# Graph attention, experts and slice attention on one core: chain rows are scattered to a table with one row per node, and router scores are made from raw rows

## The chip, the cores and the metric

One core of a Trainium2 chip runs the whole program. The metric is the device time of one execution in microseconds (us). The engines are PE (TensorE), DVE (VectorE), ACT (ScalarE), POOL (GpSimd) and SP (SyncE); SP, ACT and POOL also issue transfers (DMAs).

## The reference

Two layers, each a graph stage and a dense stage, on 3125 nodes of 256 features, with 50,000 edges sorted by destination:

```python
# layer 0, graph: attention over edges, 8 heads of 32, plus a self loop per node
e = leaky_relu(a_src[src] + a_dst[dst], 0.2)
e = exp(e - segment_max(e, dst)[dst])
alpha = e / segment_sum(e, dst)[dst]
out = segment_sum(xh[src] * alpha, dst) + bias
out = (out - mean(out, 0)) * rsqrt(var(out, 0) + eps) * gamma + beta
x = x + out + ...                                      # residuals
# layer 0, dense: router over 8 experts, top 2 of softmax
xn = layernorm(x); probs = softmax(xn @ router_w.T)
x = x + sum over the top 2 experts of gate * w2(silu(w1 xn) * w3 xn)
# layer 1: sums of source rows per node, then slice attention
```

## The kernel before, in words

The program is a row of blocks, each of which ends with a barrier of all engines: `first_phase`, `spread_phase`, `edge_phase`, `join_phase`, `router_phase`, `experts_phase`, and then the second layer. Inside a block each engine's order is written out by hand, and semaphores tie them together. `me(dve, ...)` is a step on DVE that waits for its own end before the next.

The edges are cut into ET = 392 tiles of 128 (EP). `edge_phase` makes for every edge position running sums within its tile and stores them in the table `parts` (272 numbers a row: 256 sums, 8 denominators, 8 maxima). A node whose edges end in a tile has its sums in one row of `parts`, the main row; if its edges began in an earlier tile, what came before has to be carried over tile borders.

`join_phase` does that. It loads the last row of every tile (`lasts`), lays them out with 8 heads or 128 features on the partitions, runs scans over the 392 tiles on DVE (maxima, denominators, sums), and turns the result back into `carried`, 98 x 4 rows. Before the change `carried` is stored as `chains`, 392 rows and one neutral row. POOL gathers for each node its main row (25 indirect DMAs of 125 nodes, `join_main`) and then its chain row (25 more, `join_chain`); a node without a chain reads the neutral row. The node's own message (`join_xh`, `own`) and its main row are weighted and added first, with weights of their own (`early`, in PSUM), then chain rows come in and all is rescaled. Five groups of TB = 5 tiles of 125 nodes (P) make up the 25 tiles (NT); one DVE instruction handles a group, 1280 elements. Then mean and variance over nodes are summed on PE with a matrix of ones, and the features go into the residual `res`.

`move` issues a transfer over 125 partitions as two DMAs, of 120 and of 5 partitions.

`router_phase` takes statistics of `res` (`norm_stats`), makes normalized rows (`r_xn`) on DVE, stores them for the experts (`xn_tab`), and per node tile turns the rows on PE, copies them on ACT and multiplies by the turned router weights (`rwt`): `logits`. Softmax, top 2 and the slot lists of the experts follow on DVE.

`first_phase` makes the row numbers (`main_row`, `chain_row`, `start_row`) at its end. `spread_phase` has POOL scatter and gather (25 + 4 + 28 indirect DMAs) while PE and ACT turn the first expert's weights (`w_raw`, `w_stage`).

Of the kernel before, what the change touches and what calls it, by code (L numbers as in the profile page):

```python
# [40 lines left out]
NO_CHAIN = ET  # L41
# [64 lines left out]
def setup(k):  # L106
# [28 lines left out]
    k.chains = k.dram("chains", [ET + 1, RW])  # L135
# [9 lines left out]
def first_tables(k, ctx):  # L145
# [3 lines left out]
    k.chain_rows = k.sb("chain_row", [128, NT], I32, ctx)  # L149
# [7 lines left out]
    k.main_row, k.chain_row = k.main_rows[0:P, :], k.chain_rows[0:P, :]  # L157
# [8 lines left out]
def first_phase(k):  # L166
# [4 lines left out]
    with ctx:  # L171
# [15 lines left out]
        last_i, has, t0, t1 = sb("last_i", [P, NT], I32), sb("has", [P, NT]), sb("t0", [P, NT]), sb("t1", [P, NT])  # L187
# [40 lines left out]
        def _(sp):  # L228
# [20 lines left out]
            sp.dma_start(k.chains[NO_CHAIN:NO_CHAIN + 1, :], dummy[:, :]).then_inc(dummies_out, 16)  # L249
            sp.wait_ge(dummies_out, 32)  # L250
# [33 lines left out]
        def _(pool):  # L284
# [7 lines left out]
            for rows in (tiles_i[:, :], k.main_rows[:, :], k.chain_rows[:, :], k.places[:, :, :]):  # L292
                nc.gpsimd.memset(rows, 0)
# [57 lines left out]
        def _(dve):  # L351
# [66 lines left out]
            for t in range(NT):  # L418
# [11 lines left out]
            me(dve, v.tensor_copy(last_i[:, :], last[:, :]))  # L430
            me(dve, v.tensor_single_scalar(tile_i[:, :], last_i[:, :], 7, ALU.logical_shift_right))
            me(dve, v.tensor_copy(tile[:, :], tile_i[:, :]))


            v.tensor_scalar(t0[:, :], last[:, :], -float(NO_ROW), None, ALU.add)
            me(dve, v.scalar_tensor_tensor(out=t1[:, :], in0=tile[:, :], scalar=float(EP), in1=start[:, :],
                                           op0=ALU.mult, op1=ALU.is_gt))
            v.tensor_tensor(t0[:, :], t0[:, :], has[:, :], ALU.mult)
            me(dve, v.tensor_tensor(t1[:, :], t1[:, :], has[:, :], ALU.mult))
            v.tensor_scalar(k.main_row[:, :], t0[:, :], float(NO_ROW), None, ALU.add)  # L440
            me(dve, v.tensor_scalar(tile[:, :], tile[:, :], -1.0 - NO_CHAIN, None, ALU.add))
            me(dve, v.tensor_tensor(t1[:, :], t1[:, :], tile[:, :], ALU.mult))
            v.tensor_scalar(k.chain_row[:, :], t1[:, :], float(NO_CHAIN), None, ALU.add)
# [134 lines left out]
def spread_phase(k):  # L578
# [4 lines left out]
    with ctx:  # L583
# [4 lines left out]
        own0 = sb("own0", [P, NT, H])  # L588
        firsts_in = k.gather_sem("firsts_in")
# [6 lines left out]
        @block.sync  # L596
        def _(sp):
            for m in range(3):
                w.load(sp, 0, NE - 1, m)
            for m in range(3):  # L600
                w.store(sp, 0, NE - 1, m)
                w.load(sp, 1, 0, m)
            sp.wait_ge(starts_out, 16 * NT)
            sp.dma_start(sparse[:, :], edge_rows).then_inc(sparse_in, 16)

# [27 lines left out]
        def _(act):  # L633
            act.wait_ge(w.cleared, 1)
# [8 lines left out]
        def _(dve):  # L643
            v = nc.vector
            w.clear()
            st["dve"](dve, v.tensor_tensor(own0[:, :, :], k.xh[:, :, C:C + H], k.xh[:, :, C + H:RW], ALU.add))
# [495 lines left out]
def gather_rows(pool, into, table, row, rows_in):  # L1142

    for t in range(NT):
# [4 lines left out]
def join_phase(k):  # L1149
# [7 lines left out]
    w = RW  # L1157
    with ctx:
# [4 lines left out]
        sum_t = [sb(f"sum_t{c}", [128, ET]) for c in range(2)]  # L1163
        den_t, max_t, den_c, max_c, neg, keep, scale = (sb(n, [H, ET]) for n in ("den_t", "max_t", "den_c", "max_c", "neg", "keep", "scale"))
        xh = sb("xh", [P, NT, C])
        mains, chains = sb("main", [128, NT, RW]), sb("chain", [128, NT, RW])
        main, chain = mains[0:P, :, :], chains[0:P, :, :]
        top1, top, tmp = sb("top1", [P, NT, H]), sb("top", [P, NT, H]), sb("tmp", [P, NT, H])
        den1, den = sb("den1", [P, NT, H]), sb("den", [P, NT, H])
        gap, wt = sb("gap", [P, 2, NT, H]), sb("wt", [P, 2, NT, H])  # L1170
        rowv = sb("rowv", [P, 2, C])
        mean, var = sb("mean", [P, C]), sb("var", [P, C])
        mains_in, chains_in = k.gather_sem("join_mains_in"), k.gather_sem("join_chains_in")
        lasts_in, turned, drops, factors, spread, scanned, back, rows_made, stored = (
            sem(n) for n in ("lasts_in", "turned", "drops", "factors", "spread", "scanned", "back", "rows_made", "stored"))
# [4 lines left out]
        early = k.ps[5][0:P, 0:2 * NT * H].rearrange("p (a t h) -> p a t h", a=2, h=H)  # L1180
# [1147 lines left out]
```

## Time and profile before

| | us |
|---|---|
| median of three runs | 2132.3 (2129.28 to 2139.41) |
| the profiled execution | 2129.41 |
| its span | 2127.5 |
| PE busy | 1339.4 (63%) |
| DVE busy | 926.3 (44%) |
| POOL busy | 1127.4 (53%) |
| join, from its start to its end | 666 to 808 |
| router | 808 to 894 |
| experts | 894 to 1270 |

The profiled execution took 1.9 us more than its span, which is what lies around it, and 2.9 us less than the median. The stages follow from the barriers between the blocks. In a row of a timeline the bracket at its end is the time for which the engine had been idle and what ended that.

### The profile page before, as it was taken

What the parts mean: (1) busy time and instruction counts of PE and PEld (TensorE: products, weight loads), DVE (VectorE), ACT (ScalarE), POOL (GpSimd) and SP (SyncE); (2) the same over time, 40 slices, a digit from 0 to 9 for tenths busy, and PEclk for the clock granted to TensorE, in tenths of its full rate; (3) what the DMA queues carried; (4) which work ended last, traced back from release to release, by engine and by line L of the source; (5) the groups of instructions that cost most, each with busy time, mean ns of one, the idle gap of its engine ahead of it and who ended that gap; (6) DMA issues with size and microseconds to landing.
All of it is one profiled execution on the core that took longest, in us unless ns stands there. A gap on an engine that the chain in (4) does not pass through costs nothing. (4 is left out here: it accounts for less than half of the span.)

```text
span 2127.5 us, 23423 instructions
## 1 busy us (share of the span) xinstructions
PE 1339.4 (63%) x6378; PEld 1096.7 (52%) x6378; DVE 926.3 (44%) x1854; ACT 436.9 (21%) x1241; POOL 1127.4 (53%) x1105
## 2 busy tenths in 40 slices
PE   2612666656663155399999995055656566587878
PEld 1412544444443045399999995044444444464557
DVE  8613443454452675733333333733333333255543
ACT  0112544334442012133333331000000000012210
POOL 3376777777774600277322372177777777703320
PEclk6756888777776575599999997577778777789999
DMA  5444998888888703143111023633333333300002
GB/s 133 129 132 133 299 309 259 277 286 291 265 281 226 107 0 102 28 143 94 42 47 69 28 95 81 169 105 105 104 107 104 107 104 105 105 11 0 0 1 60
DMA packets 150672, 268.29 MB, mean 126 GB/s; under 512 B 23662, under 2 KB 112186, under 8 KB 149437
## 3 DMA queue, kind: packets, MB, share of 16 engines
q0 software_dynamic: 47136, 126.92, 20.9%
q1 hardware_dynamic: 89985, 126.37, 18.3%
q10 hardware_dynamic: 13438, 13.56, 3.0%
q8 instruction: 63, 1.03, 0.2%
q14 instruction: 50, 0.41, 0.1%
HBM read 172.94 MB, written 94.74 MB: 126 GB/s over the span
## 5 line engine op out<-in xcount | busy, mean ns | idle before, releaser
L1080 POOL DMA_INDIRECT sum_rows<-xn_tab,src_e x392 | 371.7, 948 | 174.2 <-issue 116.1
L1101 PE MATMUL bank<-sum_rows,sum_hot 128*125 x896 | 291.1, 496 | 257.3 <-SPq L1071 241.5
L721 POOL DMA_INDIRECT gat_rows<-xh_tab,src_e x364 | 348.1, 956 | 116.2 <-issue 109.1
L1101 PEld LDWEIGHTS bank<-sum_rows,sum_hot 128*125 128x125 f32 x896 | 218.2, 252 | 327.4 <-issue 282.8
L793 PE MATMUL bank<-gat_rows,gat_same 128*128 128x264 f32 x784 | 267.6, 483 | 138.4 <-issue 138.4
L793 PEld LDWEIGHTS bank<-gat_rows,gat_same 128*128 128x128 f32 x784 | 175.5, 243 | 179.2 <-issue 148.1
L1127 DVE TENSOR_TENSOR sums<-sums,bank 125x256 f32 x224 | 94.4, 421 | 337.1 <-PE bank L1101 334.8
L1688 PE MATMUL bank<-weights,e_xthigh 128*128 x896 | 220.5, 330 | 8.3 <-DVE e_xtlow L1805 5.4
L837 ACT COPY gat_outs<-bank 128x264 f32<-128x264 f32 x392 | 148.5, 380 | 249.5 <-PE bank L793 243.5
L1810 DVE TENSOR_TENSOR e_h<-e_gated,bank 128x342 f32<-128x342 f32 x112 | 57.1, 510 | 263.2 <-ACT e_gated L1758 263.2
L1688 PEld LDWEIGHTS bank<-weights,e_xthigh 128*128 128x128 f32 x896 | 154.2, 192 | 18.1 <-issue 17.9
L1688 PE MATMUL bank<-weights,e_xtlow 128*128 x448 | 144.9, 324 | 0.0
L1709 PE MATMUL bank<-weights,e_hthigh 128*128 (+2 forms) x672 | 133.5, 294 | 0.3 <-DVE e_htlow L1815 0.3
L758 DVE TENSOR_TENSOR gat_rows<-gat_rows,bank 128x1792 f32<-128x1792 f32 x56 | 110.4, 2013 | 0.5 <-ACT bank L829 0.5
L1592 POOL CAST weights<-staged 128x4264 fp32r<-128x4264 f32 x7 | 26.3, 3761 | 152.0 <-SPq L1637 143.0
L1709 PEld LDWEIGHTS bank<-weights,e_hthigh 128*128 128x128 f32 (+2 forms) x672 | 102.6, 189 | 0.5 <-issue 0.5
L1758 ACT ACTIVATE e_gated<-bank 128x342 f32<-128x342 f32 x112 | 51.0, 456 | 239.8 <-PE bank L1688 239.8
L1709 PE MATMUL bank<-weights,e_htlow 128*128 x336 | 94.1, 280 | 0.0
L1688 PEld LDWEIGHTS bank<-weights,e_xtlow 128*128 128x128 f32 x448 | 85.8, 192 | 0.0
L742 DVE TENSOR_TENSOR gat_logit<-gat_rows,adst_e 128x112 f32<-128x112 f32 x28 | 7.7, 276 | 153.4 <-DMA gat_rows<-xh_tab,src_e 153.4
L2032 POOL TENSOR_TENSOR t_logit<-t_logit,t_peak 125x512 f32<-125x512 f32 x25 | 26.1, 1045 | 82.7 <-DVE t_peak L2191 82.7
L1653 POOL DMA_INDIRECT y_tab<-e_x,slot_row x52 | 50.6, 973 | 34.7 <-ACT e_x L1768 20.3
(463 smaller groups left out, 2303.2 us busy)
## 6 DMA issues: line engine op xcount, KB each, us to landing
parts<-gat_outs SPq DMA_DIRECT2D x28, 1904.0 KB, 8.1
staged<-w_tab SPq DMA_DIRECT2D x8, 2132.0 KB, 8.4
w_tab<-w_stage SPq DMA_DIRECT2D x16, 682.0 KB, 10.5
w_raw<-in_L_ffn_w_dram SPq DMA_DIRECT2D x16, 640.0 KB
gat_rows<-xh_tab,src_e POOLq DMA_INDIRECT x392, 4.5
sum_rows<-xn_tab,src_e POOLq DMA_INDIRECT x392, 2.8
w_tab<-w_stage SPq DMA_DIRECT2D x8, 768.0 KB, 10.5
w_raw<-in_L_ffn_w_dram SPq DMA_DIRECT2D x8, 682.0 KB, 11.3
```

Of the source, the lines that this page charges most:

```text
L721: pool.indirect_dma_start(out=rows[b % R][:, t, :], out_offset=None, in_=k.xh_tab, in_offset=bass.IndirectOffsetOnAxis(ap=k.src_e[:, b * S ...
L758: v.tensor_tensor(f, f, weight[b % 2][:, t0 * H:t1 * H].rearrange("p (t h a) -> p t h a", h=H, a=1).to_broadcast([EP, SB // 2, H, D]), ALU ...
L793: nc.tensor.matmul(k.ps[1 + n % BK][:, 0:sums_w], same[b % 2][:, t, :], rows[b % R][:, t, 0:sums_w], start=True, stop=True).then_inc(sums, 1)
L837: nc.scalar.copy(outs[b % 2][:, t, 0:sums_w], k.ps[1 + n % BK][:, 0:sums_w]).then_inc(taken, 1)
L1080: pool.indirect_dma_start(out=rows[:, at // IP % (RING * GPAIRS), at % IP, :], out_offset=None, in_=k.xn_tab, in_offset=bass.IndirectOffse ...
L1101: m = nc.tensor.matmul(k.ps[s][0:P, 0:C], hot[u][:, s, c, :], rows[:, bass.ds(slot, 1), c, :].rearrange("p a c -> p (a c)"), start=(c == 0 ...
L1127: v.tensor_tensor(into, into, k.ps[s][0:P, 0:C], ALU.add).then_inc(added, 1)
L1653: pool.indirect_dma_start(out=k.y_tab, out_offset=bass.IndirectOffsetOnAxis(ap=k.slot_row[:, i:i + 1], axis=0), in_=k.x_row(i), in_offset= ...
L1688: last = nc.tensor.matmul(bank[:, 0:HH[a]], xt[s][px][:, c, :], part(slot, up_at(m, pw, c) + HB[a], 128, HH[a]), start=(n == 0), stop=(n = ...
L1709: m = nc.tensor.matmul(DOWN[s][:, 0:C], ht[a][ph][0:rows, b, :], part(slot, down_at(pw, 3 * a + b), rows, C), start=(a == 0 and n == 0), s ...
L1758: nc.scalar.activation(gated[a][:, 0:HH[a]], UP[a][:, 0:HH[a]], ACT.Silu).then_inc(silued, 1)
L1810: v.tensor_tensor(h[a][:, 0:HH[a]], gated[a][:, 0:HH[a]], GATE[a][:, 0:HH[a]], ALU.mult).then_inc(h_made, 1)
```

## The change

1. The table `chains` is gone. In its place is `node_chain`, one row for each of the 3125 nodes. ACT fills it in `spread_phase` with neutral rows, from an SBUF row `empty` (3125 rows of 1088 bytes, 3.4 MB). `join_phase` scatters `carried` to it, four indirect DMAs on POOL, and then loads it whole into `join_chain` with plain DMAs: tiles 0 to 12 from SP, 13 to 24 from ACT.
2. The node that each tile's chain belongs to (`chain_node`) is found in `spread_phase` by two matmuls, nine short DVE steps on one partition, four transposes and a copy. `first_phase` loses the eight DVE instructions for `chain_row`, a memset and one small DMA.
3. POOL issues 18 gathers of main rows, waits for `carried`, issues the four scatters, then the other 7 gathers.
4. The early weights are gone: all three terms get their weights once chain rows are there, with one exponential of 600 columns instead of two of 400.
5. The load of `join_xh` waits for `lasts`.
6. The router weights are loaded in the join, centred over their columns and turned at its head. The scores are made from raw rows of `res` at the end of the join, group by group behind the last DVE passes, and are multiplied by `rstd` in the router. The statistics move into the join too, and ACT's square root for them stands behind its 25 copies.
7. The normalized rows are made on ACT in the router, after the exponential, 25 instructions, instead of on DVE.

```diff
 # spread_phase
+            act.wait_ge(empty_made, 2)
+            move(act, k.node_chain.rearrange("(t p) c -> p t c", p=P), empty[:, :].rearrange("p (a c) -> p a c", a=1).to_broadcast([P, NT, RW]), k.chain_cleared)
             act.wait_ge(w.cleared, 1)
...
+            me(dve, v.tensor_tensor(whole[:, :], whole[:, :], follows[:, 1:1 + ET], ALU.mult))
+            me(dve, v.tensor_scalar(whole[:, :], whole[:, :], -1.0, 1.0, ALU.mult, ALU.add))
+            me(dve, v.tensor_tensor(whole[:, :], whole[:, :], follows[:, 0:ET], ALU.mult))
...
 # join_phase, sync
+            sp.dma_start(rw[:, :], k.a["L0_ffn_router_w"]).then_inc(rw_in, 16)
...
-            sp.wait_ge(rows_made, 1)
-            sp.dma_start(k.chains[0:ET, 0:w].rearrange("(q j) c -> q j c", j=J), carried[:, :, :]).then_inc(stored, 16)
+            sp.wait_ge(stored, 16 * J)
+            move(sp, chain[:, 0:SPLIT, :], node_rows[:, 0:SPLIT, :], chains_in)
 # gpsimd
-            gather_rows(pool, mains, k.parts[:, :], k.main_rows, mains_in)
-            pool.wait_ge(stored, 16)
-            gather_rows(pool, chains, k.chains[:, :], k.chain_rows, chains_in)
+            gather_rows(pool, mains, k.parts[:, :], k.main_rows, mains_in, range(FIRST_MAINS))
+            pool.wait_ge(rows_made, 1)
+            for j in range(J):
+                pool.indirect_dma_start(out=k.node_chain, out_offset=bass.IndirectOffsetOnAxis(ap=k.chain_node[:, j:j + 1], axis=0),
+                                        in_=carried[:, j, :], in_offset=None, bounds_check=N - 1, oob_is_err=False).then_inc(stored, 16)
+            gather_rows(pool, mains, k.parts[:, :], k.main_rows, mains_in, range(FIRST_MAINS, NT))
 # tensor, behind the two sums over nodes
+            pe.wait_ge(rw_ready, 1)
+            for t in range(NT + 1):
+                if t < NT:
+                    if t % TB == 0:
+                        pe.wait_ge(grown, t // TB + 1)
...
+                        m = nc.tensor.transpose(k.ps[2 + t % XR][:, c * P:(c + 1) * P], k.res[:, t, c * 128:(c + 1) * 128], k.ident[0:P, 0:P])
...
+                        m = nc.tensor.matmul(logits[:, (t - 1) * NE:t * NE], xt[:, (t - 1) % XR, c, :], rwt[:, c, :], start=(c == 0), stop=(c == 1))
 # vector
+            dve.wait_ge(rw_in, 16)
...
+            dve.wait_ge(beta_kept, 1)
+            v.tensor_tensor(k.res[:, :, :], k.res[:, :, :], beta.rearrange("p (a c) -> p a c", a=1).to_broadcast([P, NT, C]), ALU.add)
             dve.wait_ge(mains_in, 16 * NT)
...
+            dve.wait_ge(chains_in, 64)
...
+            me(dve, v.tensor_tensor(wt[:, :, :, :], wt[:, :, :, :], den[:, :, :].rearrange("p (a t) h -> p a t h", a=1).to_broadcast([P, 3, NT, H]), ALU.mult))
...
-                v.tensor_tensor(heads(main[:, tiles, 0:C]), heads(main[:, tiles, 0:C]), by_head(wt[:, 0, tiles, :]), ALU.mult)
-                me(dve, v.tensor_tensor(heads(chain[:, tiles, 0:C]), heads(chain[:, tiles, 0:C]), by_head(wt[:, 1, tiles, :]), ALU.mult))
+                me(dve, v.tensor_tensor(heads(chain[:, tiles, 0:C]), heads(chain[:, tiles, 0:C]), by_head(wt[:, 2, tiles, :]), ALU.mult))
...
-                m = v.tensor_tensor(k.res[:, tiles, :], k.res[:, tiles, :], feat, ALU.add)
-            me(dve, m)
+                v.tensor_tensor(k.res[:, tiles, :], k.res[:, tiles, :], feat, ALU.add).then_inc(grown, 1)
+            dve.wait_ge(grown, BODIES)
+            norm_stats(k, dve, deviations, roots)
 # router_phase, scalar
+            for t in range(NT):
+                nc.scalar.activation(xn1[:, t, :], k.res[:, t, :], ACT.Identity, bias=shift[:, t:t + 1], scale=k.rstd[:, t:t + 1]).then_inc(made, 1)
 # router_phase, vector
+            me(dve, v.tensor_tensor(prob[:, :, :], scores, wide(k.rstd), ALU.mult))
```

Three places in the engines' orders are shown, before and after. The first is POOL in `join_phase`, with the barriers around it (the last `ISA` rows clear semaphores). Before:

```order
L1191 UNCONDITIONAL_BRANCH [waits barrier_Pool_Activation_PE_DVE_SP_gather]
L1145 DMA join_main<-parts,main_row 128x272 x25
L1145 DMA join_chain<-chains,chain_row 128x272 [waits join_stored]
L1145 DMA join_chain<-chains,chain_row 128x272 x24
L1197 ISA x56
L1158 UNCONDITIONAL_BRANCH
```

After:

```order
L1219 UNCONDITIONAL_BRANCH [waits barrier_Pool_Activation_PE_DVE_SP_gather]
L1163 DMA join_main<-parts,main_row 128x272 x18
L1224 DMA node_chain<-join_carried,chain_node 3125x272 [waits join_rows_made]
L1224 DMA node_chain<-join_carried,chain_node 3125x272 x3
L1163 DMA join_main<-parts,main_row 128x272 x7
L1228 ISA x60
L1177 UNCONDITIONAL_BRANCH
```

The 25 chain gathers behind the wait for the stored table are gone; four scatters stand in their place, and 7 gathers of main rows have moved behind them.

The second is ACT at the head of `join_phase`: first the load of `join_xh`, then the two exponentials that the scans need (`join_keep`, `join_scale`). Before:

```order
L141 DMA join_xh<-xh_tab 120x25x256
L142 DMA join_xh<-xh_tab 5x25x256
L1235 ACTIVATE join_keep<-join_keep 8x392 [waits join_drops]
L1236 ACTIVATE join_scale<-join_scale 8x392
L1239 COPY bank<-join_rowv 125x256 [waits join_scanned,join_vecs_in]
L1241 ACTIVATE bank<-join_gap 125x400 [waits join_gaps]
L1243 ACTIVATE join_wt<-join_gap 125x400 [waits join_gaps]
```

After:

```order
L140 DMA join_xh<-xh_tab 120x25x256 [waits join_lasts_in]
L141 DMA join_xh<-xh_tab 5x25x256
L1286 ACTIVATE join_keep<-join_keep 8x392 [waits join_drops]
L1287 ACTIVATE join_scale<-join_scale 8x392
L1290 COPY bank<-join_rowv 125x256 [waits join_scanned,join_vecs_in]
L140 DMA join_chain<-node_chain 120x12x272 [waits join_stored]
L141 DMA join_chain<-node_chain 5x12x272
L1294 ACTIVATE join_wt<-join_gap 125x600 [waits join_gaps]
```

The load of `join_xh` now stands behind a wait for `lasts`, still ahead of the exponentials, and ACT's half of the chain rows stands ahead of the weights' exponential.

The third is PE at the border of join and router: the end of the second sum over nodes, then the router's transposes (`ident` with rows) and scores (`rwt` with turned rows). Before:

```order
L1228 MATMUL bank<-join_chain,ones 125x256 [waits join_squared]
L1228 MATMUL bank<-join_chain,ones 125x256 x4
L1158 UNCONDITIONAL_BRANCH
L1413 UNCONDITIONAL_BRANCH [waits barrier_Pool_Activation_PE_DVE_SP_release]
L1417 MATMUL bank<-ident,r_rw 128x8 [waits r_rw_in]
L1417 MATMUL bank<-ident,r_rw 128x8
L1427 MATMUL bank<-ident,r_xn 128x125 [waits r_made,r_rw_ready]
L1427 MATMUL bank<-ident,r_xn 128x125
L1427 MATMUL bank<-ident,r_xn 128x125 [waits r_made]
L1427 MATMUL bank<-ident,r_xn 128x125
L1432 MATMUL bank<-r_rwt,r_xt 125x8 [waits r_kept]
L1432 MATMUL bank<-r_rwt,r_xt 125x8
```

After:

```order
L1263 MATMUL bank<-join_chain,ones 125x256 [waits join_squared]
L1263 MATMUL bank<-join_chain,ones 125x256 x4
L1273 MATMUL bank<-ident,res 128x125 [waits join_grown,join_rw_ready]
L1273 MATMUL bank<-ident,res 128x125 x3
L1278 MATMUL bank<-join_rwt,join_xt 125x8 [waits join_res_kept]
L1278 MATMUL bank<-join_rwt,join_xt 125x8
L1273 MATMUL bank<-ident,res 128x125 x2
L1278 MATMUL bank<-join_rwt,join_xt 125x8 [waits join_res_kept]
L1278 MATMUL bank<-join_rwt,join_xt 125x8
```

The barrier between the sum and the first transpose is gone, and the transposes read `res` and wait for `grown`, the count of groups that DVE has finished, instead of normalized rows.

## Rows read from the trace of the kernel before

**Rows 1.** Busy time by stage: engine busy us (instructions), PEclk, DMA share, GB/s.

```profile
666.00:808.00 142.00, 38.77 (x140) 28.54 (x140) 93.51 (x85) 10.42 (x12) 50.58 (x51) 0.61 0.45 80
808.00:894.00 86.00, 43.40 (x206) 41.47 (x206) 55.17 (x161) 11.16 (x29) 4.87 (x10) 0.50 0.25 69
```

**Rows 2.** Timeline of POOL in the join: start us, us, instruction, [idle before <-releaser].

```profile
667.56 0.95 POOL L1145 DMA_INDIRECT join_main<-parts,main_row  x1 [25.32 <-POOLq L676]
...
698.20 0.96 POOL L1145 DMA_INDIRECT join_main<-parts,main_row  x1 [0.30 <-issue]
704.61 0.95 POOL L1145 DMA_INDIRECT join_chain<-chains,chain_row  x1 [5.45 <-DMA chains<-join_carried]
```

**Rows 3.** Timeline of ACT at the head of the join.

```profile
667.27 16.80 ACTq L142 DMA_DIRECT2D join_xh<-xh_tab  x1
685.75 0.53 ACT L1235 ACTIVATE join_keep<-join_keep 8x392 f32<-8x392 f32 x1 [26.41 <-DVE join_scale L1270]
```

**Rows 4.** Timeline of DVE in the join, to the last pass over node rows.

```profile
682.09 0.85 DVE L1255 COPY join_max_t<-bank 8x392 f32<-8x392 f32 x1 [14.78 <-PE bank L1204]
...
688.28 0.55 DVE L1276 TENSOR_TENSOR join_keep<-join_keep,joins 8x392 f32<-8x392 f32 x1
...
698.93 0.42 DVE L1288 COPY join_carried<-bank 98x32 f32<-98x32 f32 x2
...
744.40 0.37 DVE L1310 TENSOR_TENSOR join_top<-join_top,join_chain 125x200 f32<-125x200 f32 x1 [10.32 <-DMA join_chain<-chains,chain_row]
...
749.17 1.49 DVE L1321 TENSOR_TENSOR join_main<-join_main,join_wt 125x1280 f32<-125x1280 f32 x1
...
769.42 1.49 DVE L1323 TENSOR_TENSOR join_main<-join_main,join_chain 125x1280 f32<-125x1280 f32 x1
```

**Rows 5.** Timeline of PE, sum over the joined rows.

```profile
753.65 7.59 PE L1228 MATMUL bank<-join_main,ones 125*125 125x256 f32 x20 [54.70 <-DVE join_main L1323]
...
770.96 2.42 PE L1228 MATMUL bank<-join_main,ones 125*125 125x256 f32 x10 [1.91 <-DVE join_main L1323]
```

**Rows 6.** Timeline of DVE, end of the join and head of the router.

```profile
792.67 1.49 DVE L1342 TENSOR_TENSOR join_main<-join_main,join_var 125x1280 f32<-125x1280 f32 x1
...
807.94 8.27 DVE L453 BATCH_NORM_STATS2 stats<-res 125x6 f32<-125x256 f32 x25 [0.54 <-PEq L1158]
...
818.08 8.17 DVE L1348 TENSOR_SCALAR r_xn<-res,mv,rstd 125x256 f32<-125x256 f32 x25
848.16 0.37 DVE L1477 TENSOR_REDUCE r_peak<-bank 125x25 f32<-125x200 f32 x1 [21.91 <-PE bank L1432]
```

**Rows 7.** Timeline of PE, first transposes of the router.

```profile
818.64 1.06 PE L1427 MATMUL bank<-ident,r_xn 125*128 125x125 f32 x4 [8.90 <-DVE r_xn L1348]
```

**Rows 8.** Timeline of DVE, end of the first phase.

```profile
92.59 0.18 DVE L430 CAST last_i<-last 125x25 int32<-125x25 f32 x1
...
94.89 0.18 DVE L446 TENSOR_SCALAR start_row<-t 125x25 int32<-125x25 f32 x1
```

**Rows 9.** Timeline of POOL in the spread phase.

```profile
96.47 2.17 POOL L609 DMA_INDIRECT adst_edge<-xh,start_row  x1 [31.80 <-issue]
98.95 1.21 POOL L609 DMA_INDIRECT adst_edge<-xh,start_row  x1 [0.31 <-issue]
...
177.03 0.96 POOL L616 DMA_INDIRECT gat_rows<-xh_tab,src_e  x1 [0.30 <-issue]
```

**Rows 10.** Timeline of ACT, last copies of the spread phase.

```profile
155.41 5.95 ACT L640 COPY adst_e<-bank 128x392 f32<-128x392 f32 x8 [45.63 <-PE bank L629]
```

**Rows 11.** Busy time by stretch, chosen for its DMA share and GB/s.

```profile
7.00:26.00 19.00, 5.97 (x24) 4.38 (x24) 16.75 (x43) 1.28 (x1) 0.00 (x0) 0.82 0.96 186
667.00:684.00 17.00, 2.77 (x16) 2.24 (x16) 2.15 (x5) 0.00 (x0) 12.48 (x14) 0.50 0.99 224
705.00:738.00 33.00, 0.00 (x0) 0.00 (x0) 28.84 (x18) 0.00 (x0) 25.69 (x25) 0.50 0.81 90
100.00:118.00 18.00, 8.90 (x36) 6.76 (x36) 0.00 (x0) 4.86 (x12) 14.34 (x13) 0.50 0.97 310
```

More of the change, by code:

```diff
@@ L40 @@
 NO_ROW = ET * EP
-NO_CHAIN = ET
 BIG = 3e38
@@ L291, in _ @@
             nc.gpsimd.iota(k.lane[:, :], pattern=[[1, EP]], base=0, channel_multiplier=0, allow_small_or_imprecise_dtypes=True)
[L292 removed]
+            for rows in (tiles_i[:, :], k.main_rows[:, :], k.places[:, :, :]):
                 nc.gpsimd.memset(rows, 0)
@@ L429, in _ @@
             me(dve, v.tensor_scalar(last[:, :], end[:, :], -1.0, 0.0, ALU.add, ALU.max))
[L430 to L443, printed above, removed]
+            me(dve, v.tensor_scalar(t0[:, :], last[:, :], -float(NO_ROW), None, ALU.add))
+            me(dve, v.tensor_tensor(t0[:, :], t0[:, :], has[:, :], ALU.mult))
+            me(dve, v.tensor_scalar(k.main_row[:, :], t0[:, :], float(NO_ROW), None, ALU.add))
             me(dve, v.tensor_scalar(t0[:, :], start[:, :], -float(NO_ROW + 1), None, ALU.add))
@@ L620, in _ @@
         def _(pe):
+            nc.tensor.matmul(k.ps[0][0:1, 0:ET], k.ident[:, 0:1], k.dst_e[:, :], start=True, stop=True)
+            nc.tensor.matmul(k.ps[1][0:1, 0:ET], k.ident[:, EP - 1:EP], k.dst_e[:, :], start=True, stop=True).then_inc(ends_found, 1)
             for m in range(3):
@@ L1139, in _, with gather_rows @@
             add(ITURNS - 1, 1)
-def gather_rows(pool, into, table, row, rows_in):
-    for t in range(NT):
+def gather_rows(pool, into, table, row, rows_in, tiles):
+    for t in tiles:
         pool.indirect_dma_start(out=into[:, t, :], out_offset=None, in_=table,
@@ L1172, in join_phase @@
+        res_turned, res_kept, scored, deviations, roots = (k.sem(f"join_{n}") for n in ("res_turned", "res_kept", "scored", "deviations", "roots"))
+        logits = k.ps[5][0:P, 0:NT * NE]
         mean, var = sb("mean", [P, C]), sb("var", [P, C])
-        mains_in, chains_in = k.gather_sem("join_mains_in"), k.gather_sem("join_chains_in")
-        lasts_in, turned, drops, factors, spread, scanned, back, rows_made, stored = (
-            sem(n) for n in ("lasts_in", "turned", "drops", "factors", "spread", "scanned", "back", "rows_made", "stored"))
+        mains_in, stored = k.gather_sem("join_mains_in"), k.gather_sem("join_stored")
@@ L1176, in join_phase @@
+        chains_in = k.sem("join_chains_in")
+        lasts_in, turned, drops, factors, spread, scanned, back, rows_made = (
+            sem(n) for n in ("lasts_in", "turned", "drops", "factors", "spread", "scanned", "back", "rows_made"))
         xh_in, vecs_in, beta_kept, gaps, weights, joined, summed, centred, squared, dev, root = (
@@ L1200, in _ @@
         def _(pe):
+            pe.wait_ge(rw_centred, 1)
+            for c in range(2):
+                m = nc.tensor.transpose(k.ps[6][:, c * NE:(c + 1) * NE], rw[:, c * 128:(c + 1) * 128], k.ident[0:NE, 0:NE])
+            m.then_inc(rw_turned, 1)
             pe.wait_ge(lasts_in, 16)
@@ L1239, in _ @@
             nc.scalar.copy(beta, rowv[:, 1, :]).then_inc(beta_kept, 1)
+            act.wait_ge(stored, 16 * J)
+            move(act, chain[:, SPLIT:NT, :], node_rows[:, SPLIT:NT, :], chains_in)
             act.wait_ge(gaps, 1)
-            nc.scalar.activation(early, gap[:, :, :, :], ACT.Exp).then_inc(weights, 1)
-            act.wait_ge(gaps, 2)
             nc.scalar.activation(wt[:, :, :, :], gap[:, :, :, :], ACT.Exp).then_inc(weights, 1)
@@ L1449, in _ @@
         def _(act):
-            norm_roots(k, act, deviations, roots)
-            for t in range(NT):
-                act.wait_ge(turned, t + 1)
-                if t >= XR:
-                    act.wait_ge(multiplied, t - XR + 1)
-                nc.scalar.copy(xt[:, t % XR, :, :].rearrange("p a n -> p (a n)"), k.ps[t % XR][:, 0:2 * P]).then_inc(kept, 1)
             act.wait_ge(less_peak, 1)
             nc.scalar.activation(prob[:, :, :], prob[:, :, :], ACT.Exp).then_inc(exped, 1)
+            act.wait_ge(shifts_made, 1)
+            for t in range(NT):
+                nc.scalar.activation(xn1[:, t, :], k.res[:, t, :], ACT.Identity, bias=shift[:, t:t + 1], scale=k.rstd[:, t:t + 1]).then_inc(made, 1)
         @block.vector
```

154 lines of the change are left out of this document (84 added, 70 removed).

## The prediction

> **What bounds the kernel now.** I read the busy time by stage first, then the timelines of each engine inside the join and the router. The change touches 228 us of the span, the join (142 us) and the router (86 us), plus the end of the first phase and the spread phase, which lie between 92 and 183 us. In the join no engine is busy for long: DVE for 93.5 of 142 us, POOL for 50.6, and DMA engines for 0.45 of it [rows 1]. So the stage is a chain, and the bracket behind each row says what it waits for.
>
> The chain through the join is: `lasts` lands and is turned, DVE starts at 682.09, having waited 14.78 us [rows 4]; scans until `carried` is complete at 698.93 + 0.42 = 699.35 [rows 4]; the table is stored and POOL starts the 25 chain gathers at 704.61 [rows 2]; the last lands and DVE goes on at 744.40, after 10.32 us of idling [rows 4]. DVE's work on main rows fits inside that wait. Then 15 passes to 769.42 + 1.49 = 770.91 [rows 4], two sums on PE, and the last DVE passes from 792.67 [rows 6]. In the router DVE makes statistics and normalized rows (8.27 and 8.17 us), then idles 21.91 us for PE until 848.16 [rows 6]: PE's loop of transposes and scores, which began at 818.64 [rows 7], is the bound there, 29.5 us.
>
> **Part by part.** All against the profiled 2129.41 us.
>
> *End of the first phase.* The row numbers are made in dependent steps from 92.59 to 94.89, 13 gaps in 2.30 us [rows 8]. Eight instructions go, and five gaps of about 0.2 remain, 1.1 us. POOL's first scatter waits for this. Term: -1.2.
>
> *Spread phase.* POOL sets its end: 57 indirect DMAs without a pause, the last at 177.03 [rows 9]; ACT ends at 155.41 + 5.95 = 161.4 [rows 10]. New matmuls and short DVE steps go into DVE's idle time. The 3.4 MB of neutral rows are added to a stretch whose DMA share is 0.97 at 310 GB/s [rows 11]: 11 us more of transfer. ACT issues them first, and a second DMA behind a large one held ACT for 16.80 us in the join [rows 3], so the copies of turned weights, and behind them SP's stores and loads, start up to 17 us late. That is covered by 178.0 - 161.4 = 16.6 us, and more, since the `sparse` load waits for scatters rather than for ACT. What can lengthen POOL is DVE: the first scatter took 2.17 us beside DVE's clearing of `w_stage`, the next 1.21 [rows 9]. Two small memsets join that one, and three short steps have two operands in SBUF. From nothing to 3 us; I take +1.0, what one such scatter lost.
>
> The Trainium skill (Advanced Engine Details and Errata, Miscellaneous Facts, GPSIMD Details) says that Pool shares an interface with DVE and conflicts with DVE instructions that have two SBUF inputs. By that rule the three steps cost POOL their own length, 1.6 us if each takes the 0.55 of such a product [rows 4], instead of 1.0; the long first scatter fits it.
>
> *Head of the join.* `lasts` no longer shares the DMA engines with `join_xh`. The stretch moved 224 GB/s at a share near 1 [rows 11]; 0.43 MB beside POOL's gathers should land about 5.5 us after the block's start at 667, at 672.5, 8 us earlier. Centring and turning the router weights costs some 2 us of that. But ACT now issues `join_xh` at 672.5 and is held by its second DMA: 16.80 us before [rows 3], less the 1.9 us that 0.43 MB took at 224 GB/s, so until 687.8. The exponentials stand behind it (685.75 before [rows 3]), and DVE needed both for its row at 688.28 [rows 4]: now 688.9. So the 8 us are not collected, and `carried` is ready at 700.0 instead of 699.35. Bounds: if ACT is held for nothing, `carried` comes up to 6 us earlier; if `lasts` lands at 675, 2 us later.
>
> *From `carried` to chain rows.* POOL's first 18 main gathers end at 667.56 + 18 x 1.28 = 690.6 [rows 2], so it waits for `carried`. No row shows a scatter of 1088-byte rows; between the gather step of 1.28 us [rows 2] and the scatter step 98.95 - 96.47 = 2.5 at worst [rows 9], I take 1.5: issued by 706, landed by 709.5. Then 3.4 MB of chain rows, with 0.7 MB of main rows left. Rates for such rows [rows 11]: 186 GB/s in the load of `x` on one queue (from 7 to 26 us), 224 with `join_xh`, `lasts` and gathers on three (667 to 684); 310, among the weights' loads and stores, isn't for such rows alone. I take 235: 17.5 us. Chain rows complete at T = 727.5 (718 to 735), instead of 744.40. The `beta` pass goes into DVE's wait.
>
> *Behind T.* Before, from 744.40 to 770.91: 26.5 us, of which 4.8 for weights and 21.7 for 15 passes [rows 4]. Now the weights take 5.9 (two more short steps of 0.4, wider exponential and product), the 15 passes of own and main rows 21.7, and ten of chain rows 14.7, which is what ten such passes take from 792.67 to the statistics less a barrier of 0.54 [rows 6]. Sum 42.3, to 769.8. Term: 769.8 - 770.9 = -1.1. Equal would be T = 728.6.
>
> *Sum on PE.* It needed 7.59 us for the first two groups, and 2.42 a group after that, at 0.38 and 0.24 us a matmul [rows 5]. Groups now come every 2.9 us rather than 4.3, so it ends 3.1 behind DVE instead of 2.5. Term: +0.6.
>
> *End of the join and router.* Before, from 792.67 to 848.16: 55.5 us [rows 6]. Now the first group of `res` is there after 2 passes, 2.95 us; then PE's loop, 29.5 (its 25 turns are slower than DVE's groups, so PE waits only for the first); DVE's passes and statistics (14.7 + 8.3 = 23 us) fit beside it; the barrier 0.54 and one more DVE step 0.4. Sum 33.4. ACT's square root behind its copies ends about with PE. Term: -22.1, the greatest; between -20, if ACT's square root and DVE's reciprocal stick out, and -23.
>
> *Normalized rows on ACT.* 25 instructions of 256 columns at about the 0.38 us of such a copy, 9 us from 829, and a store of 3.2 MB, 18 us at one queue's rate: done near 856. Experts' rows are gathered when the slot lists are ready, near the router's end, which was 894 and becomes 872. Hidden by 8 us or more. Term 0.
>
> Sum: -1.2 + 1.0 - 1.1 + 0.6 - 22.1 = -22.8, to 2106.6 for a run like the profiled one. The median of the runs shown is 2.9 above that run: **2109.5 us**.
>
> **The rivals.**
>
> *Chain rows come sooner* (0.15). ACT isn't held, `carried` comes 4 us earlier, and both queues reach 310 GB/s: 13.2 us. T = 718.7, 8.8 less: 2100.7. For it: the 310 [rows 11]. Against: no stretch of 1 KB reads shows it. [...]
>
> *The neutral fill spills over* (0.12). ACT's hold, at 16.80 us or more, with the fill's competition for the DMA engines, delays the turned weights and `adst_e` beyond POOL's end. It decides from 16.6 us of lateness in ACT's last copies; with 25 us it costs 8: 2117.5.
>
> *The scores don't leave the path* (0.05). If PE's loop were slowed beside DVE's and ACT's work, or effectively began behind the statistics, the 22 us would be gone: about 2131.5, no change.
>
> *Slower: chain rows load at the rate of the old chain gathers* (0.04). From 705 to 738 the DMA engines were 0.81 busy with 90 GB/s [rows 11]. 4.1 MB at 90 GB/s take 46 us and 4 more for the scatters' tail: T = 759.5, 32 us after the forecast: 2141.5. It decides from T = 750, where all is lost. Against it: most of those gathers read one neutral row over and over, and now each node has its own; `join_xh`, laid out the same way, came faster.
>
> **How the numbers follow.** The forecast as worked out, T between 722 and 733, has 0.62: 2104 to 2115. With the rivals at 0.15, 0.12, 0.05 and 0.04 (0.02 for the rest), the range takes in the sooner load and the spill: 2099 to 2120. This kernel can be told from no change at about 0.5%, 10.7 us, below 2121.6: faster 0.62 + 0.15 + 0.12 = 0.89 and half of the rest, 0.90; same 0.06; slower 0.04.
>
> **What would show it.** Spread phase: POOL's last gather within 3 us of 177 - 1.2, ACT busy issuing at its head. Join: DVE's first copy of maxima near 676, but its product after the exponentials near 689, with ACT as releaser; `carried` near 700; the step that waits for chain rows near 727; PE's sums near 773; scores ending 56 to 57 us after that; the router's first DVE step near 825. The prediction is wrong if the plain loads run above 300 or below 150 GB/s, if ACT's hold is short, or if PE's loop per tile grows beyond 1.15 us.

## The result, and the profile after

Before 2130.99 us (median of 4 runs, one more than in the table of the kernel before, 2129.28 to 2139.41), after **2103.89 us** (4 runs, 2102.44 to 2105.96): 27.1 us less, ratio 0.9871 with a 95% interval of 0.9855 to 0.9888. The forecast was 2109.5 in a range of 2099 to 2120. Between the two profiled executions the difference is 2129.41 - 2105.96 = 23.45 us; the forecast for that pair was 22.8.

Busy time by stage after, to be read against [rows 1]: the spread phase's head, join and router. The third line is the router, 46 us where it was 86; the scores are in the join, which nevertheless took 157 us, against 142 with no scores in it.

```profile
100.00:118.00 18.00, 9.40 (x40) 7.20 (x40) 2.83 (x8) 4.77 (x12) 14.47 (x12) 0.54 1.00 277
669.00:826.00 157.00, 66.67 (x292) 56.96 (x292) 96.68 (x119) 19.40 (x37) 28.13 (x29) 0.59 0.30 72
826.00:872.00 46.00, 13.58 (x54) 12.20 (x54) 37.90 (x103) 13.94 (x27) 5.16 (x10) 0.50 0.49 129
```

DVE's timeline of the join, against [rows 4, 6]:

```profile
674.40 0.41 DVE L1324 TENSOR_REDUCE join_rw_mean<-join_rw 8x1 f32<-8x256 f32 x1 [4.33 <-DMA join_rw<-in_L_ffn_router_w_dram]
...
677.24 0.85 DVE L1312 COPY join_max_t<-bank 8x392 f32<-8x392 f32 x1 [1.22 <-PE bank L1239]
...
690.60 0.55 DVE L1342 TENSOR_TENSOR join_keep<-join_keep,joins 8x392 f32<-8x392 f32 x1 [7.23 <-ACT join_scale L1287]
...
701.25 0.42 DVE L1354 COPY join_carried<-bank 98x32 f32<-98x32 f32 x2
...
729.38 0.37 DVE L1363 TENSOR_TENSOR join_top<-join_top,join_chain 125x200 f32<-125x200 f32 x1 [7.90 <-DMA join_chain<-node_chain]
...
770.22 1.49 DVE L1384 TENSOR_TENSOR join_main<-join_main,join_chain 125x1280 f32<-125x1280 f32 x1
774.23 0.42 DVE L1387 TENSOR_SCALAR join_mean<-bank 125x256 f32<-125x256 f32 x1 [2.52 <-PE bank L1263]
...
793.24 1.49 DVE L1403 TENSOR_TENSOR join_main<-join_main,join_var 125x1280 f32<-125x1280 f32 x1
...
808.00 8.26 DVE L443 BATCH_NORM_STATS2 stats<-res 125x6 f32<-125x256 f32 x25
...
826.21 0.37 DVE L1506 TENSOR_TENSOR r_prob<-bank,rstd 125x200 f32<-125x200 f32 x1 [0.93 <-PEq L1177]
826.61 0.36 DVE L1507 TENSOR_REDUCE r_peak<-r_prob 125x25 f32<-125x200 f32 x1
```

Times are best taken from the start of the join, when SP issues the load of `lasts`: 666.91 before, 669.21 here. T is the start of the DVE step that waits for the last chain row. DVE reads the first maxima 8.0 us after that, where it took 15.2 [rows 4]. That lead is gone at 690.60, where DVE waits for ACT. `carried` is complete at 701.67, 32.5 us from the start, before 32.4. Chain rows are there at T = 729.38, 60.2 us from the start, before 77.5. The last pass over node rows ends at 771.71. From 793.24 to the router's peaks at 826.61 there are 33.4 us, where there were 55.5 [rows 6].

ACT's and PE's timelines, against [rows 3, 5, 7]:

```profile
674.42 15.08 ACTq L141 DMA_DIRECT2D join_xh<-xh_tab  x1
689.55 0.53 ACT L1286 ACTIVATE join_keep<-join_keep 8x392 f32<-8x392 f32 x1 [27.91 <-issue]
...
824.44 0.37 ACT L1304 COPY join_xt<-bank 128x250 f32<-128x250 f32 x1 [0.79 <-PE bank L1273]
...
827.74 12.38 ACT L1493 ACTIVATE r_xn<-res,r_shift,rstd 125x256 f32<-125x256 f32 x25
```

```profile
760.05 8.40 PE L1263 MATMUL bank<-join_main,ones 125*125 125x256 f32 x30 [58.80 <-DVE join_main L1384]
...
771.77 2.42 PE L1263 MATMUL bank<-join_main,ones 125*125 125x256 f32 x10 [0.51 <-DVE join_main L1384]
...
796.40 1.06 PE L1273 MATMUL bank<-ident,res 125*128 125x125 f32 x4 [6.35 <-DVE res L1404]
```

ACT stood at the second load of `join_xh` for 15.08 us and its exponentials ran after it. PE begins on raw rows of `res` at 796.40, one group behind DVE, and ACT makes its last copy of the 25 at 824.44.

POOL's timeline, in the join and where the experts begin, against [rows 2]; the first gather of the experts stood at 886.73 before:

```profile
702.59 1.01 POOL L1224 DMA_INDIRECT node_chain<-join_carried,chain_node  x1 [10.12 <-DVEq L1355]
...
706.48 0.96 POOL L1224 DMA_INDIRECT node_chain<-join_carried,chain_node  x1 [0.30 <-issue]
707.74 1.00 POOL L1163 DMA_INDIRECT join_main<-parts,main_row  x1 [0.30 <-issue]
...
865.22 0.99 POOL L1614 DMA_INDIRECT x_head<-xn_tab,slot_token  x1 [37.69 <-DVEq L1577]
```

### The profile page after: what moved, and what is told of

It reads as the page before. It is cut to its first block and busy times, and to the rows that moved or that the text cites. A ratio compares the mean times of both kernels' runs of the same rounds, so it can differ in the third digit from the quotient of the medians.

```text
span 2104.2 us, 23418 instructions
## 1 busy us (share of the span) xinstructions
PE 1346.7 (64%) x6386; PEld 1101.9 (52%) x6386; DVE 915.4 (44%) x1835; ACT 448.6 (21%) x1265; POOL 1105.8 (53%) x1083
```

## The experiments

Times are told from the start of the join, since the edge phase ahead of it, the same code in all versions, put that start anywhere between 663.96 and 669.21 us (786 to 802 us in the last four runs, on a slower chip). "Peaks" is the router's `r_peak` step: 157.4 us from the start in the changed kernel, 181.25 before.

### One half of the change at a time

`scores_only` keeps the table `chains`, its gathers and the two-step weights; `table_only` keeps the scores and the normalized rows in the router. Cores of the two edits, each against the changed kernel:

```diff
 # scores_only
-            move(sp, chain[:, 0:SPLIT, :], node_rows[:, 0:SPLIT, :], chains_in)
...
+            sp.dma_start(k.chains[0:ET, 0:w].rearrange("(q j) c -> q j c", j=J), carried[:, :, :]).then_inc(stored, 16)
...
+            gather_rows(pool, chains, k.chains[:, :], k.chain_rows, chains_in)
 # table_only
-            pe.wait_ge(rw_ready, 1)
-            for t in range(NT + 1):
...
+            dve.wait_ge(multiplied, NT)
...
+            me(dve, v.tensor_reduce(peak[:, :], scores, AX, ALU.max))
```

> Only the scores, the statistics and the normalized rows are moved as in the change; chain rows are gathered as before. My theory, that the greatest term stands by itself: 21 to 23 us less than the kernel before, about 2107.5, and about 3 us more than the change. Rival, that the gain is made of both parts together (PE's loop hides only because the rest of the join is shorter): 10 to 15 us less than before. In the profile the first router step on DVE should come some 33 us after the last DVE passes begin, as after the change.

Measured: 2108.14 us (6 runs), ratio 0.9874 (0.9848 to 0.9900), 23.3 us below the 2131.41 of the kernel before on that chip.

> Only the chain table, its load whole, the order of the gathers and the single set of weights; statistics, normalized rows and scores stay in the router as before. My theory: 2 to 3 us less than before, about 2127 (the end of the first phase 0.9, the joined rows 1.5 earlier against the join's start). Rival, that the table is worth most of what the run gained beyond my forecast: 5 us or more less than before. The other rival, that the table costs time and the scores hide it: more than before.

Measured: 2127.95 us (12 runs), ratio 0.9974 (0.9958 to 0.9991), 3.5 us less. The two add up to 26.7 of the 27.1 us, but the intervals are 5.5 us to either side for `scores_only` and 3.5 for `table_only`, so they show no gain that only both together make, to within some 6 us. DVE's timelines, `scores_only` first, then `table_only`:

```profile
746.54 0.37 DVE L1348 TENSOR_TENSOR join_top<-join_top,join_chain 125x200 f32<-125x200 f32 x1 [10.66 <-DMA join_chain<-chains,chain_row]
...
828.19 0.36 DVE L1484 TENSOR_REDUCE r_peak<-r_prob 125x25 f32<-125x200 f32 x1
```

```profile
723.34 0.37 DVE L1330 TENSOR_TENSOR join_top<-join_top,join_chain 125x200 f32<-125x200 f32 x1 [7.69 <-DMA join_chain<-node_chain]
...
842.87 0.37 DVE L1505 TENSOR_REDUCE r_peak<-bank 125x25 f32<-125x200 f32 x1 [21.92 <-PE bank L1460]
```

In `scores_only` chain rows arrive 78.4 us from the start (668.17), as before. In `table_only` they arrive at 58.4 (start 664.90), and DVE still waits 21.92 us for PE's scores. The scores are the gain; the table is a small one (1.9 to 9.0 us by its interval), since what it wins at T it pays behind T.

### What holds the head of the join: `small_first` and `xh_on_sp`

```diff
 # small_first, scalar: the DMA over 5 partitions ahead of the one over 120
-            move(act, xh[:, :, :], k.xh_tab.rearrange("(t p) c -> p t c", p=P)[:, :, 0:C], xh_in)
+            xh_rows = k.xh_tab.rearrange("(t p) c -> p t c", p=P)[:, :, 0:C]
+            act.dma_start(xh[MOST:P, :, :], xh_rows[MOST:P]).then_inc(xh_in, 16)
+            act.dma_start(xh[0:MOST, :, :], xh_rows[0:MOST]).then_inc(xh_in, 16)
 # xh_on_sp: the same load from SP
+            sp.wait_ge(lasts_in, 16)
+            move(sp, xh[:, :, :], k.xh_tab.rearrange("(t p) c -> p t c", p=P)[:, :, 0:C], xh_in)
```

> The changed kernel, with the two DMAs of the join_xh load in the other order: 5 partitions first, then 120. Theory: ACT is held because the second DMA's issue waits for room behind the large one; with the large one last, ACT is free in under 1 us, the exponentials run when DVE's differences are ready (near 681 instead of 689.6), carried and chain rows come 6 to 8 us earlier, and the time is 6 to 7 us under that of the change, about 2098. Rival: ACT's queue is held whichever DMA comes last, or the chain is then bound by the transfers (218 GB/s from 674 on): 0 to 2 us.

Measured: 2099.50 us (6 runs), ratio 0.9844 (0.9818 to 0.9870).

> The changed kernel, with join_xh loaded by SP behind the same wait for lasts, so that SP is held and not ACT. SP has nothing to do until the scattered rows are stored. Theory: the same gain as with the other order of ACT's DMAs, 6 to 7 us, about 2098. Rival, that the exponentials aren't late through the hold but through the transfers: no gain. If this one gains and the other order doesn't, ACT is held by any large DMA.

Measured: 2101.92 us (6 runs), ratio 0.9851 (0.9825 to 0.9877). ACT's timeline in `small_first`, and SP's in `xh_on_sp`:

```profile
670.50 0.26 ACTq L1285 DMA_DIRECT2D join_xh<-xh_tab  x1
670.79 0.36 ACTq L1286 DMA_DIRECT2D join_xh<-xh_tab  x1
677.37 0.53 ACT L1288 ACTIVATE join_keep<-join_keep 8x392 f32<-8x392 f32 x1 [19.32 <-DVE join_scale L1338]
```

```profile
671.58 13.77 SPq L141 DMA_DIRECT2D join_xh<-xh_tab  x1
```

With the load of all 25 tiles, the second DMA of the pair holds the engine that issues it when the large one stands first, on either engine: 15.08 us on ACT, 13.77 on SP, and 0.36 when the small one goes first. That doesn't make the hold the same everywhere. In the changed kernel SP and ACT issue their halves of the chain rows together, and the second DMAs held them for very different times, which no run explains:

```profile
709.35 0.83 SPq L141 DMA_DIRECT2D join_chain<-node_chain  x1
709.37 7.80 ACTq L141 DMA_DIRECT2D join_chain<-node_chain  x1
```

With the hold ahead of the exponentials gone, `carried` was complete 25.4 us from the start (32.5):

```profile
690.55 0.42 DVE L1356 COPY join_carried<-bank 98x32 f32<-98x32 f32 x2
```

The peaks stood at 152.6 (157.4). Of 7.1 us won at `carried`, 4.9 reached T (55.25 for 60.2) and 4.8 the peaks, less than the 6 to 7 expected of the whole: from the first scatter to the issue of the loads 9.0 us passed instead of 6.4. The scatters were issued at the same pace and landed later; they now run while `join_xh` and main rows are still moving, which may be the reason, but no run separates it. In `xh_on_sp` `carried` was complete at 24.8, yet T came only at 57.9 and the peaks at 153.7, since the chain load took 22.8 us there instead of 20.4. So the cause of the late exponentials is shown, and the expected 6 to 7 us were not reached in either; in time the two lie 4.4 and 2.0 us under the change, with intervals that overlap its own.

### What sets the rate of the chain load: `one_queue` and `mains_first`

```diff
 # one_queue (and no load on ACT)
-            move(sp, chain[:, 0:SPLIT, :], node_rows[:, 0:SPLIT, :], chains_in)
+            move(sp, chain[:, :, :], node_rows, chains_in)
 # mains_first, on top of small_first
-    FIRST_MAINS, SPLIT = 18, 13
+    FIRST_MAINS, SPLIT = 25, 13
```

> All 30 tiles of the chain rows are loaded by SP's one queue; ACT issues no load there, and its 7.80 us hold ahead of the exponentials falls away. Everything else is the changed kernel. Theory that the rate belongs to each queue (early loads on one queue moved 186 GB/s, on two 224): the load takes some 24 us instead of 20.4, T (the last chain row's arrival at DVE's wait) comes 3.5 us later, 63.7 us after the join's start, and the time is about 3.5 us above the changed kernel's. Rival, that the DMA engines shared with the main rows and their descriptors set it: T stays within 1 us of 60.2 us after the join's start, and the time is the same.

Measured: 2104.60 us (4 runs), ratio 0.9874 (0.9840 to 0.9908). `change_again`, the changed kernel on the same chip:

> The changed kernel once more, on the chip and among the runs of the three others: 2104 us, within 3 us. It is what their times are compared with.

Measured: 2103.55 us (4 runs), ratio 0.9862 (0.9828 to 0.9897).

> The small load of the node features first, as in small_first, and in addition all 25 gathers of main rows issued before the 4 chain scatters (18 before and 7 behind in the changed kernel). Theory that the 7 gathers behind the scatters take DMA time from the chain load: the scatters are issued about 7 us later, the load runs alone and takes about 4 us less than the 20 us it has now, and T comes 58 us after the join's start, against 55.25 in small_first. Rival, that POOL and not the DMA queues set the load's start: scatters wait for the gathers that stand before them in any case (small_first: the loads were issued 9.0 us after the first scatter, the changed kernel's 6.4 us), so T stays at 55 to 56 and the time within 1 us of small_first's 2099.5 us.

Measured: 2101.42 us (4 runs), ratio 0.9859 (0.9825 to 0.9894). Stretches from the issue of the loads to T, with DMA share and GB/s as the last two columns: the changed kernel, `one_queue`, `mains_first`:

```profile
708.97:729.38 20.41, 0.00 (x0) 0.00 (x0) 0.37 (x1) 0.00 (x0) 5.76 (x6) 0.50 0.87 215
```

```profile
704.22:729.21 24.99, 0.00 (x0) 0.00 (x0) 0.37 (x2) 0.00 (x0) 5.75 (x6) 0.50 0.85 175
```

```profile
703.06:722.96 19.90, 0.00 (x0) 0.00 (x0) 0.00 (x0) 0.00 (x0) 0.00 (x0) 0.50 0.83 171
```

One queue took 24.99 us for the 25 tiles (the expectation's 30 is a slip) where two took 20.41, and T stood 64.1 us from the start instead of 59.4 in `change_again`: one queue alone is slower than two. The two kernels also differ in the number of large DMAs, one or two, which no run separates. In time it showed as 1.05 us only, where 3.5 were expected; the ranges of the two overlap. But the theory that seven gathers beside the load slow it fell: in `mains_first` the load had the DMA engines to itself and took 19.90 us, at 171 GB/s in place of 215. So the 1 MB of main rows beside it costs the load 0.5 us at most. The only effect was that loads were issued later: T at 59.0 instead of 55.25, peaks at 156.5 instead of 152.6. The rival, T at 55 to 56, fell with it.

### A better version that gave its gain back: `early_weights`

```diff
 # vector, ahead of the wait for chain rows, as in the kernel before
+                v.tensor_tensor(heads(xh[:, tiles, :]), heads(xh[:, tiles, :]), by_head(early[:, 1, tiles, :]), ALU.mult)
+                me(dve, v.tensor_tensor(heads(main[:, tiles, 0:C]), heads(main[:, tiles, 0:C]), by_head(early[:, 0, tiles, :]), ALU.mult))
```

> mains_first, and in addition the weights in two steps as the kernel before has them: the sum over main and own rows while the chain rows are on their way, and only the chain rows' share behind T. Theory: behind T stand 26.5 us of the kernel before instead of 42.3, main rows are there 38 us after the join's start, the first half fits into the 18 us before T, and the joined rows are ready about 88 us after the join's start where small_first has 97.6: about 2091 us. Rival, that the early passes are not done at T (15 passes of about 1.1 us behind two exponentials, from 45 us after the start on, end at 64): then only about 6 us are gained against mains_first, about 2095 us.

Measured: 2101.41 us (4 runs), ratio 0.9857 (0.9823 to 0.9891): no gain on `mains_first`. DVE's timeline:

```profile
709.93 0.36 DVE L1370 TENSOR_TENSOR join_den<-join_main,bank 125x200 f32<-125x200 f32 x1 [4.91 <-ACT bank L1297]
...
732.33 0.37 DVE L1380 TENSOR_TENSOR join_top<-join_top,join_chain 125x200 f32<-125x200 f32 x1
...
813.98 0.36 DVE L1516 TENSOR_REDUCE r_peak<-r_prob 125x25 f32<-125x200 f32 x1
```

The peaks stand 146.7 us from the start (667.28), 9.8 us better than in `mains_first`, although the early passes ended only at 732.33, 65 us from the start, after the chain rows had come (DVE doesn't wait for them). That is the rival's mechanism, though it put the gain at 6 us. Part of the delay is ACT's queue again: the first exponential stands behind ACT's half of the chain load, and DVE waited 4.91 us for it. Between the profiles of the two, the lead counted from the join's start was 9.8 us at the peaks, 11.4 at the last gather of the second layer's sums (1826.84 and 1834.94), 10.2 at the first scores of the slice attention (1881.19 and 1888.04), 7.3 at its last ones (2006.53 and 2010.54), and 2.6 from the product with the bias (2050.27 and 2049.57) to the end. That last stretch in `mains_first`, from the scores to the bias, and a part of it:

```profile
2010.54:2049.57 39.03, 24.80 (x124) 19.36 (x122) 15.70 (x34) 2.77 (x5) 3.08 (x3) 0.83 0.00 0
2024.69:2029.00 4.31, 4.29 (x24) 3.25 (x24) 0.00 (x0) 0.00 (x0) 0.00 (x0) 1.00 0.01 4
```

And in `early_weights`:

```profile
2006.53:2050.27 43.74, 29.51 (x124) 23.31 (x122) 15.65 (x35) 2.77 (x5) 3.08 (x3) 0.69 0.00 0
2020.00:2028.00 8.00, 7.57 (x24) 5.70 (x24) 0.39 (x1) 0.00 (x0) 0.00 (x0) 0.50 0.01 2
```

The same 124 matmuls, but PE's granted clock is 0.69 instead of 0.83, and they took 29.5 us of PE instead of 24.8. PE's timelines at the same instruction, again `mains_first` first:

```profile
2024.69 0.71 PE L2138 MATMUL bank<-t_ut,att_w_fx 128*128 128x128 f32 x4 [0.77 <-DVE t_share L2261]
```

```profile
2020.01 1.23 PE L2145 MATMUL bank<-t_ut,att_w_fx 128*128 128x128 f32 x4 [0.77 <-DVE t_share L2268]
```

From 1990 to 2015 PE was busy for 21.7 and 21.4 of the 25 us, at 1.00 in both. Its large matmuls ended at 2018.7 in `mains_first` and at 2014.7 in `early_weights`. Then come short chains of small matmuls between DVE's steps, and the clock fell in both to its lower level, 0.50 (1.2 GHz); but in `mains_first` it was back at 1.00 when these projections began, and in `early_weights` it stayed at 0.50 through them and into the next ones. The stretch is 4.7 us longer, of the 8.8 lost, and PE's busy time in it grew by as much. The other 4.1 were lost ahead of it. 1.3 of them went before the first scores, at 0.87 and 0.88, and 2.8 in the slices of the attention, at 0.99 in both; there DVE's work rose from 63.5 to 65.5 us, all of it in the steps that make normalized rows (`t_xn`, 641 ns each instead of 553). Why those took longer I can't name. All this is read from one execution of each kernel.

### Is that a matter of where the attention falls?

Four kernels went to one more chip: `early_weights` again, with 3 and with 6 idle passes of DVE on the path behind T, and `small_first` again.

```diff
 # early_plus4 (early_plus8: range(6))
+            for _ in range(3):
+                me(dve, v.tensor_tensor(heads(xh[:, 0:5, :]), heads(xh[:, 0:5, :]), by_head(wt[:, 0, 0:5, :]), ALU.mult))
```

> The same kernel as early_weights. There the router's peaks stand 146.7 us after the join's start against 156.5 in mains_first, 9.8 us earlier, and yet the two took the same time (2101.41 and 2101.42 us): in the attention behind, up to the last product with its bias, 8.7 us were lost, with PE's clock granted at 0.59 between 2020 and 2040 us where mains_first had 0.86. Theory that this belongs to where the attention falls and not to the one execution: again 2101 to 2102 us, with the same stretch at a clock near 0.6. Rival, that the profiles differed by chance: about 2092 us.

> early_weights with 3 more passes of 1.4 to 1.5 us on DVE over rows that nobody reads any more, on the path behind the chain rows: the router and all behind it stand 4.3 us later. Theory that the attention's clock depends on where it falls: the time grows by less than the 4.3 us or falls, since the stretch at 0.59 may end. Rival, that early_weights lost its gain somewhere by a wait that moves along: 4.3 us more than early_again.

> early_weights with 6 more such passes, 8.6 us on the path: the router stands 155.3 us after the join's start, where mains_first has 156.5. Theory of the clock: the attention falls where that of mains_first did, and the time is that of mains_first less 1.2 us, about 2100 us, which is less than 2 us from early_again although 8.6 us of work were added. Rival: early_again and 8.6 us, about 2110 us.

> small_first once more, beside the three: 2099.5 us, within 2 us; it was the fastest so far and is compared here with early_again on one chip.

On that chip every kernel, the one before included, took 1.16 times as long (2469.46 us before), with waits in both edge phases that the other chips' profiles don't have, and runs of one kernel lay up to 65 us apart. Measured, as medians of six runs: 2432.87, 2440.16, 2439.76 and 2436.32 us, with intervals of the ratio 0.009 to 0.013 wide. In `early_plus4` three of the six lay 38 to 65 us above its fastest, and the interval goes by the other three, whose median is 2433.05. That can't tell 4 us from 8, and the question as put stays open; `small_again` can't be set against `early_again` either. What the profiles add is the same stretch at other clocks, `early_again` and `early_plus8` (the execution profiled of `early_plus4` was one of its three long ones and can't be set beside them):

```profile
2335.63:2377.02 41.39, 26.83 (x124) 21.45 (x122) 15.51 (x35) 2.77 (x5) 3.08 (x3) 0.75 0.00 0
```

```profile
2343.50:2381.49 37.99, 23.43 (x124) 18.45 (x122) 15.52 (x35) 2.77 (x5) 3.08 (x3) 0.87 0.00 0
```

With 124 matmuls each it lasted 41.4 and 38.0 us at 0.75 and 0.87, beside 43.7 at 0.69 and 39.0 at 0.83 above: its length goes with the clock. And the clock isn't fixed by the code: `early_weights` and `early_again` are the same kernel, at 0.69 on one chip and 0.75 on another. The peaks stood 147.2 us from the join's start in `early_again` (146.7 on the first chip) and 156.1 in `small_again` (152.6).

## Why the prediction was right, step by step

*End of the first phase*, -1.2: the steps themselves shrank by 1.2 us, but they began 0.34 later, so `start_row` is made 0.86 us earlier than [rows 8].

*Spread phase*, +1.0: mis-sized. POOL's first scatter starts 0.86 us earlier and its last gather, at 176.10 against 177.03 [rows 9], 0.93 earlier, so the phase cost POOL nothing. That is a sum: 0.93 won at the first scatter, 0.2 lost at two others, 0.7 lost at a gather beside DVE's scans. POOL's timeline after, and two of DVE's rows:

```profile
95.61 1.24 POOL L603 DMA_INDIRECT adst_edge<-xh,start_row  x1 [30.87 <-issue]
97.15 1.20 POOL L603 DMA_INDIRECT adst_edge<-xh,start_row  x1 [0.31 <-issue]
...
100.16 1.32 POOL L603 DMA_INDIRECT adst_edge<-xh,start_row  x1 [0.30 <-issue]
101.78 1.26 POOL L603 DMA_INDIRECT adst_edge<-xh,start_row  x1 [0.30 <-issue]
...
144.67 1.73 POOL L610 DMA_INDIRECT gat_rows<-xh_tab,src_e  x1 [0.30 <-issue]
...
176.10 0.95 POOL L610 DMA_INDIRECT gat_rows<-xh_tab,src_e  x1 [0.30 <-issue]
```

```profile
95.41 1.34 DVE L507 MEMSET w_stage<- 128x1536 f32 x1 [0.27 <-issue]
...
100.82 0.55 DVE L658 TENSOR_TENSOR whole<-whole,follows 1x392 f32<-1x392 f32 x1
```

The two scatters beside DVE's steps with two SBUF operands took 1.32 and 1.26 us where their neighbours took 1.20, some 0.2 us together. So the rule of the Trainium skill (Advanced Engine Details and Errata, Miscellaneous Facts, GPSIMD Details), that Pool and such DVE instructions conflict, holds in direction here; the size that the prediction drew from it, the steps' own length of 1.6 us, doesn't. The term's own source, a scatter lengthened by DVE's clearing of `w_stage`, was misread: the first scatter, 2.17 us before, took 1.24 beside the same clearing. What lengthened it before no run shows. The fill was hidden, with the DMA share at 1.00 from 100 to 118: ACT was held by it for 14.59 us, and still ended the phase's copies at 160.2, before POOL.

*Head of the join*, +0.65 at `carried`: measured 0.0. That `lasts` comes 8 us sooner (DVE's first copy of maxima was 7.2 us sooner, and centring the router weights took the rest) and that the hold of ACT takes it all was right (product forecast at 688.9, 21.9 us after the start as assumed; measured 21.4), and `small_first` shows it by removing the hold.

*Chain rows*, T 60.5 us from the start: measured 60.2, by luck, since two errors cancel. Scatters took 1.3 us a step instead of 1.5 and landed sooner, so loads were issued 39.8 us from the start instead of 42.5; and the load took 20.4 us at some 215 GB/s instead of 17.5 at 235, a rate that stands in no row and was chosen between 224 and 310. Even the load that ran alone took 19.90 us.

*Behind T*, 42.3: measured 729.38 to 771.71, 42.3. *Sum on PE*, +0.6: 0.0, since it ended 2.5 us behind DVE as before. *End of join and router*, 33.4: measured 33.4. *Normalized rows on ACT*, 9 us: 12.38. The prediction took the 0.38 us of a copy; this form, with a scale and a bias per partition, took 0.50. Hidden all the same.

What I didn't foresee lies outside the change: the edge phase took 3.2 us more in the profiled run after (join start +2.3 though it began 0.9 earlier), within the 5 us by which the join's start differs between versions with the same edge phase. And from the experts' first gather to the end the span is 1.8 us shorter. So the parts that the forecast names came to -24.7 us where it had -22.8, and the two unforeseen parts, together +1.4, brought the profiled pair back to within 1 us of the forecast. That closeness is in part luck; the greatest term, -22.1, is not. The medians differ by 27.1 rather than 23.5 because the profiled execution lay 1.6 us under the median before and 2.1 above it after: spread between executions, for which the forecast has no step.

Of the rivals, chain rows sooner fell (rate 215, not 310), as did the spill and the load at 90 GB/s; that the scores stay on the path fell with the 33.4 us after the last passes began, here and in `scores_only`.

## What to carry to other kernels

A loop that is bound on one engine by latency is best laid beside another engine's passes, if algebra lets it start from unfinished rows: that gave 23 of 27 us here. When a pair of DMAs is issued from an engine that has compute behind it, issue the small one first: here it cost 15 us of ACT's time and 4.8 us at the router's peaks. And an improvement is to be measured at the end of the program as well as at its place: 9.8 us won in the join by `early_weights` were not in its time.

The fastest version measured is `small_first`, 2099.50 us against 2103.89 and 2103.55 for the change, though their intervals overlap and the medians weren't all taken on one chip; its lead is seen in the profile, 4.8 us at the peaks.

## What the runs showed of the hardware

A load of 3125 rows of about 1 KB took 20 us from two queues whether or not a third moved 1 MB beside it (171 and 215 GB/s), 22.8 in `xh_on_sp`, and 25 us as one load from one queue. The hold of the second DMA behind a load of 25 tiles of features is found on both engines (15.08 us on ACT, 13.77 on SP); behind half the chain rows it was 7.80 us on ACT and 0.83 on SP. The same 124 matmuls of the attention's middle took between 38.0 and 43.7 us at granted clocks from 0.87 to 0.69.
